# First tile of a cross-attention and FP4-FFN kernel: order of its start and placing of POOL's weight rounding

## The reference

```
x = x + xattn(layernorm(x), ctx)     # ctx (4, 154, 192), 16 heads of 64
    q = x @ Wq;  k = ctx @ Wk;  v = ctx @ Wv
    out = softmax(q k^T / 8) v;  out @ Wo + bo
x = x + ffn(layernorm(x))            # hidden size 704
    gate = fp4(x) @ fp4(w_gate)^T;  up = fp4(x) @ fp4(w_up)^T
    h = silu(gate) * up;  fp4(h) @ fp4(w_down)^T
fp4(v): scale = max|block of 16| / 6; nearest of 0, .5, 1, 1.5, 2, 3, 4, 6 times sign times scale
```

## Time and profile before

| what | us |
|---|---|
| median of 3 runs | 884.25 |
| the profiled execution | 883.6 |
| its span, first to last instruction | 881.8 |
| busy: DVE | 709.8 |
| busy: POOL | 541.3 |
| busy: ACT | 524.4 |

### The profile page before, as it was taken

How to read it: one execution, slowest core, us unless ns; L and a number is a source line. 1 busy time by engine, 2 the same in 40 slices (tenths; PEclk the granted TensorE clock), 3 DMA queues, 4 the chain that set the end, 5 groups by cost and what they waited for, 6 DMA issues and landing times.

```text
span 881.8 us, 19215 instructions
## 1 busy us (share of the span) xinstructions
PE 837.9 (95%) x6310; PEld 809.9 (92%) x6310; DVE 709.8 (80%) x2155; ACT 524.4 (59%) x1868; POOL 541.3 (61%) x810
## 2 busy tenths in 40 slices
PE   7877899999999999999999999999999999999986
PEld 6756899999988999999988999999989999999985
DVE  3888788877787888887867888887877888888887
ACT  3654566666665666666655666666665666666531
POOL 3758677764645666666553667665644567666644
PEclk7999999999999999999999999999999999999998
DMA  5301000002010000002010000000200000000000
GB/s 158 121 24 45 7 19 13 25 8 60 8 49 19 14 25 14 25 14 55 13 50 19 13 19 13 25 14 15 59 7 19 13 13 26 13 19 13 7 7 19
DMA packets 20756, 24.30 MB, mean 28 GB/s; under 512 B 2061, under 2 KB 18869, under 8 KB 20661
## 3 DMA queue, kind: packets, MB, share of 16 engines
q1 hardware_dynamic: 19573, 22.04, 8.7%
q10 hardware_dynamic: 1088, 1.05, 0.4%
HBM read 18.89 MB, written 4.19 MB: 26 GB/s over the span
## 4 chain that ended last, share of the span: by engine, by line
PE 79%; DVE 13%; issue 2%; POOL 2%; ACT 2%; DMA 1%; SPq 0%; DVEq 0%; ACTq 0%
PE ps_g L1328 12%; PE ps_s L1281 10%; PE ps_q L1235 10%; PE ps_t L1293 7%; PE ps_o L1310 7%; PE ps_o L1308 7%; PE ps_o L1309 7%; PE ps_m L1159 3%; PE ps_m L1342 3%; PE ps_m L1344 2%; PE ps_m L1343 2%; PE ps_g L1193 2%; PE ps_g L1182 2%; DVE negmax L905 2%; PE ps_q L1193 1%
## 5 line engine op out<-in xcount | busy, mean ns | idle before, releaser
L515 POOL TENSOR_TENSOR probs<-probs,rsum 128x308 f32<-128x308 f32 x256 | 180.6, 706 | 227.6 <-DVE rsum L888 227.1
L666 ACT ACTIVATE probs<-ps_s,negmax 128x154 f32<-128x154 f32 x512 | 195.1, 387 | 201.4 <-DVE negmax L905 199.8
L905 DVE TENSOR_REDUCE negmax<-ps_s 128x2 f32<-128x308 f32 x256 | 120.8, 472 | 81.1 <-PE ps_s L1281 80.3
L1308 PE MATMUL ps_o<-B_sb,pT_lo 128*128 128x256 f32 x640 | 181.3, 283 | 0.9 <-DVE x_both L1009 0.6
L1310 PE MATMUL ps_o<-B_sb,pT_hi 128*128 128x256 f32 x640 | 181.2, 283 | 0.0
L1309 PE MATMUL ps_o<-B_sb,pT_hi 128*128 128x256 f32 x640 | 180.9, 283 | 0.0
L779 DVE TENSOR_TENSOR pT_lo<-ps_t,pT_hi 128x256 fp32r<-128x256 f32 (+1 forms) x256 | 122.6, 479 | 31.3 <-ACT pT_hi L593 31.1
L1328 PE MATMUL ps_g<-WGU,xqT_hi 128*128 128x352 f32 x504 | 132.0, 343 | 1.9 <-DVE B_sb L779 1.7
L1293 PE MATMUL ps_t<-ident,probs 128*128 128x128 f32 x640 | 113.2, 275 | 13.5 <-DVE pT_lo L779 11.2
L1308 PEld LDWEIGHTS ps_o<-B_sb,pT_lo 128*128 128x128 f32 x640 | 121.3, 190 | 1.5 <-issue 0.8
L1310 PEld LDWEIGHTS ps_o<-B_sb,pT_hi 128*128 128x128 f32 x640 | 121.9, 191 | 0.0
(11 more groups left out here) (230 smaller groups left out, 2199.0 us busy)
## 6 DMA issues: line engine op xcount, KB each, us to landing
xa<-in_x_dram SPq DMA_DIRECT2D x33, 128.0 KB, 2.2
xr<-in_x_dram SPq DMA_DIRECT2D x32, 128.0 KB, 2.0
out_dram<-y_xn SPq DMA_DIRECT2D x30, 128.0 KB, 1.7
W_sb<-in_L_xattn_Wk_dram SPq DMA_DIRECT2D x3, 768.0 KB, 5.7
W_sb<-in_L_xattn_Wv_dram SPq DMA_DIRECT2D x2, 768.0 KB, 5.5
probs<-in_L_xattn_Wq_dram ACTq DMA_DIRECT2D x4, 256.0 KB, 5.5
Wo_sb<-in_L_xattn_Wo_dram SPq DMA_DIRECT2D x1, 1024.0 KB, 6.4
W_sb<-in_L_xattn_Wv_dram SPq DMA_DIRECT2D x2, 384.0 KB, 3.7
```

Of the source, the lines that this page charges most:

```text
L515: pool.tensor_tensor(unit, unit, rsum[:, 2 * u:2 * u + 2].unsqueeze(2) .to_broadcast([P, 2, M]), ALU.mult).then_inc(norm_p, 1)
L666: ins = act.activation(probs[:, h, 0:M], ps_s[k % 2][:, s * M:(s + 1) * M], ACT.Exp, bias=negmax[:, h:h + 1], accum_out=sums[:, h:h + 1])
L905: dve.tensor_reduce(negmax[:, 2 * k:2 * k + 2], ps_s[k % 2][:, 0:UM].rearrange("p (h m) -> p h m", h=2), AX_X, ALU.max, negate=True).then_ ...
L1308: pe.matmul(ps_o[:, 0:C], lo[:, j, :], w[:, 0:C], start=first, stop=False)
```

## The change

- PE runs no idle products between K's first product and the transposes of x.
- ACT and DVE split x ahead of K's first job; they had it behind.
- q of tile pair 0, unit 1, goes to the bank `ps_s[1]`, which the scores of slot 1 use later, and no longer waits for the low part of unit 0. Unit 2 now waits for the low part of unit 0, and the following units wait as before.
- POOL runs the three stages of chunks 0 to 4 in one go, one slot after RAW_AT, right behind the normalise of that slot; nothing of chunk 4 is left for the next tile's slot 0.

```
--- before.py
+++ after.py
@@ -212,6 +212,10 @@
 
         def q_slots(t, par):
             return {k: k + 2 for k in range(PAIRS - 2)} if isinstance(t, int) and t == 0 else Q_SLOTS[par]
+
+        def q_bank(pair, u):
+
+            return ps_s[1] if pair == 0 and u == 1 else ps_q
 
         def q_unit(t, par, k):
             return q_slots(t, par).get(k)
@@ -503,10 +507,10 @@
             pool.wait_ge(pre_mm, CTX_T)
             pool.memset(VT[:, :, :], 0.0).then_inc(pad_p, 1)
 
-            def round_chunk(c, stages):
+            def round_chunk(c):
                 n = RAW_N[c]
                 fp4(raw[RAW_IN[c]][:, 0:n], raw_c[c % 2][:, 0:n], raw_s[c % 2][:, 0:n // BLOCK], raw_p, 3 * c,
-                    (raw_v, 6 * c + 6), stages)
+                    (raw_v, 6 * c + 6))
 
 
             def normalise(t, u):
@@ -527,12 +531,10 @@
             def first(t, setup):
                 for k in range(SLOTS):
                     normalise(t, k)
-                    if raw_at(t, k, 2) is not None:
-                        round_chunk(raw_at(t, k, 2), (2,))
                     if t == 0 and k == 0:
                         rstd(mv1, rs1, nm1, (ln1_v, 9), ln1_p, 8)
                     if raw_at(t, k, 1) is not None:
-                        round_chunk(raw_at(t, k, 1), (0, 1))
+                        round_chunk(raw_at(t, k, 1))
                     if k == 1:
                         add_bias(t)
                     if k == 3:
@@ -552,8 +554,8 @@
                         normalise(e, PAIRS - 1)
                     if own and k >= 1:
                         normalise(t, k - 1)
-                    if raw_at(t, k, 2) is not None:
-                        round_chunk(raw_at(t, k, 2), (2,) if raw_at(t, k, 2) == raw_at(1, 0, 2) else range(3))
+                    if raw_at(t, k, 2) is not None and (t, k) != (1, 0):
+                        round_chunk(raw_at(t, k, 2))
                     if own and k == 0:
                         add_bias(t)
                     if down and 1 <= k < 4:
@@ -593,7 +595,7 @@
                 act.activation(dst, src, ACT.Copy).then_inc(done, 1)
 
             def q_hi_part(pair, u):
-                hi_part(q_sb[0][:, u, :], ps_q[:, 0:2 * P], (q_mm, PAIRS * pair + u + 1), q_hi)
+                hi_part(q_sb[0][:, u, :], q_bank(pair, u)[:, 0:2 * P], (q_mm, PAIRS * pair + u + 1), q_hi)
 
             def take_hi(job, b):
                 kind, i, bank_ = job
@@ -642,8 +644,8 @@
                 context(r)
             wq_hi_part(0)
             layer_norm1_out(1, 1)
+            hi_part(xT_all(0), parts(ps_m, 4), (xT_mm, 1), xT_hi)
             take_hi(("K", 0, FIRST_K[0]), 0)
-            hi_part(xT_all(0), parts(ps_m, 4), (xT_mm, 1), xT_hi)
             wq_hi_part(1)
             q_hi_part(0, 0)
             wq_hi_part(2)
@@ -779,7 +781,7 @@
                 dve.tensor_tensor(dst, src, hi.bitcast(F32), ALU.subtract).then_inc(done, 1)
 
             def q_lo_part(pair, u):
-                lo_part(q_sb[1][:, u, :], ps_q[:, 0:2 * P], q_sb[0][:, u, :], (q_hi, PAIRS * pair + u + 1), q_lo)
+                lo_part(q_sb[1][:, u, :], q_bank(pair, u)[:, 0:2 * P], q_sb[0][:, u, :], (q_hi, PAIRS * pair + u + 1), q_lo)
 
             def take_lo(job, b):
                 kind, i, bank_ = job
@@ -868,8 +870,8 @@
             layer_norm1(0, 0, 1)
             layer_norm1(1, 1, 1)
             wq_lo_part(0)
+            lo_part(xT_all(1), parts(ps_m, 4), xT_all(0), (xT_hi, 1), xT_lo)
             take_lo(("K", 0, FIRST_K[0]), 0)
-            lo_part(xT_all(1), parts(ps_m, 4), xT_all(0), (xT_hi, 1), xT_lo)
             wq_lo_part(1)
             q_lo_part(0, 0)
             wq_lo_part(2)
@@ -1228,11 +1230,13 @@
                     pe.wait_ge(xT_lo, pair + 1)
                 if isinstance(pair, int) and pair == 0:
                     pe.wait_ge(wq_lo, u // 2 + 1)
-                if some(PAIRS * pair + u):
+                if pair == 0 and u == 2:
+                    pe.wait_ge(q_lo, 1)
+                elif q_bank(pair, u) is ps_q and some(PAIRS * pair + u):
                     pe.wait_ge(q_lo, PAIRS * pair + u)
                 terms = [(w, x_, k) for k in range(KT) for w, x_ in ((1, 0), (0, 1), (0, 0))]
                 for i, (w, x_, k) in enumerate(terms):
-                    ins = pe.matmul(ps_q[:, 0:2 * P], Wq_sb[w][:, k, u * P:(u + 1) * P], xT[x_][:, k, :],
+                    ins = pe.matmul(q_bank(pair, u)[:, 0:2 * P], Wq_sb[w][:, k, u * P:(u + 1) * P], xT[x_][:, k, :],
                                     start=(i == 0), stop=(i == len(terms) - 1))
                 ins.then_inc(q_mm, 1)
 
@@ -1255,7 +1259,6 @@
             context_transposes(range(2))
             pe.wait_ge(pre_ev, 2)
             make(("K", 0, FIRST_K[0]), 0)
-            warm(4)
             pe.wait_ge(xln1_a, 2)
             m_free(None, (xT_lo, 1))
             both_transposes(ps_m)
```

## The result

The changed kernel takes 877.54 us, the median of 4 runs (876.86 to 878.03), against 885.01 for the kernel before measured beside it (four runs): a ratio of 0.9918, 95% interval 0.990 to 0.9936. On two other chips the same kernel gave 0.9941 (0.9923 to 0.9959) and 0.9948 (0.9934 to 0.9961). So it is faster by 0.5 to 0.8%, some 5 to 7 us. The direction held; two terms of the sum were too small.

What follows compares the result with a forecast made beforehand. TensorE (PE), busy 838 of 881.8 us, was taken to pace the steady tile pairs. The front's 2.1 us plus 2.0 us from rounding in one go made 4.1, taking the median from 884.25 to about 880.1; range 877.9 to 883.0.

Steps and rivals of the forecast that it cites:

- the front: First tile up to DVE's second maximum: that maximum moves from 27.25 to 25.15, a gain of 2.1 us.
- the collision: Slots 7 and 8: DVE's scaling of chunk 5's maxima starts inside POOL's multiplication of chunk 4 and is blocked, 0.87 us lost.
- K 0's end and the half clock: First tile: K 0 still ends at 11.17; transposes and q products run at half clock, which rises near 17.5.
- the upper bound: First tile: full clock throughout, DVE's own queue sets the first maximum near 17.7, and the gain there is 3.0 us.
- The clock rival: First tile: the clock rises at 12.95 after all, gain 3.0 + 2.0 to 2.9, time 878.8; chance 0.15.
- The second bank: First tile: q 1 no longer waits for the subtraction of q 0, so 1.01 us go.
- Slots 7 and 8: Chunk 3's earlier multiplication removes DVE waits of 1.69 and 1.21 us (2.90); less 0.87 blocked, gain 2.0 us.
- Slot 5's wait: Slot 5: PE loses its 1.63 us wait for chunk 2, worth nothing because DVE had not been idle.
- The lead stays: After the first tile: a microsecond gained stays gained unless a later wait is pinned to something else.
- The slower rival: Five moved POOL multiplications each block a DVE step by 1.24 us, 6.2 lost against 5.0 gained: 885.4; chance 0.08.

Runs made afterwards that it cites:

- cold: The changed kernel without the 12 idle products at its very start: 880.12 us, ratio 0.9957.
- one_bank: The changed kernel with q 1 back in the bank of q 0: 881.11 us, ratio 0.9962.
- nudge_long: The changed kernel with a DVE clear of 512 columns ahead of the scaling of chunk 5's maxima: 877.94 us, one run.
- filled_6: The changed kernel with idle products in two PE waits, 6 ahead of K 0 and 5 ahead of q 0: 877.40 us, ratio 0.9925.
- after_third: The changed kernel, unchanged, measured again beside filled_6 and nudge_long: 879.19 us, ratio 0.9948.
- filled: The changed kernel with idle products in two PE waits, 8 ahead of K 0 and 5 ahead of q 0: 877.69 us, ratio 0.9927.
- idle_back: The changed kernel with the four idle products back ahead of the transposes of x: 879.94 us, ratio 0.9940.
- nudge: The changed kernel with a DVE clear of 64 columns ahead of the scaling of chunk 5's maxima: 878.96 us, ratio 0.9937.
- front_only: The changed kernel with POOL's rounding as in the kernel before: 881.33 us, ratio 0.9956.
- before_filled: The kernel before with idle products in the same two PE waits as the changed kernel's filled variants: 883.60 us, ratio 0.9991.

## Why the prediction was wrong

Two terms of the sum failed: the front (2.1 us forecast, 4.3 measured) and the collision (0.87 us lost by forecast, nothing measured).

- **K 0's end and the half clock: what failed in the front.** The forecast held that "K 0 still ends at 11.17: it waits for a load that is untouched", and ran the transposes and the q products at half. The wait for Wk is untouched, but the level of the clock belongs to the execution and not to the kernel: K 0 ended at 10.29. With x transposed in 0.66 instead of 1.11 us, q 0 in 0.99 instead of 1.64 and the K products in 1.21, the front gave 4.32 us where 2.1 stood: 3.72 of them by the first maximum (1.65 forecast), 0.60 from there to the second (0.43 forecast). Even the upper bound, 3.0, kept K 0's half-clock end; adding 0.88 and 0.45 us gives 4.3. cold, whose K 0 and q 0 have the lengths of the half clock, returned the forecast's front within 0.2 us: the steps were right, the level was not. The other side of the subtraction had the same fault. The profile of before had caught a full stretch from 12.95 to 16.35 us; with the half clock throughout, the old front takes 18.9 us and not 18.1, and the order is worth 3.1 us. By this comparison the rest of the 4.3 is luck of the two executions that were profiled. One step inside was also off: PE did not run on unbroken behind q 0, it waited 0.83 us for q 0's low part ahead of the scores.
- **The clock rival** was given 0.15 and priced too low for the same reason. In the first profile after the clock never fell in the front, which is more than the rival supposed; in the three profiles of the changed kernel K 0 was at full clock each time, q in two of three. Why a level is met is only in part shown: PE was idle 2.05 and 2.33 us ahead of K 0 in the two profiles of the kernel before, 1.13 to 1.46 in the three of the changed one, and that pause hangs on the landings of context and Wk; but one_bank had 2.56 us there, nudge_long 2.19, and K 0 at full clock. How often either kernel meets the half level is left open. The Trainium skill, "TensorE: Matmul & The Clock Gate", Part 1, holds that idleness brings the throttle back. filled_6's profile agrees (pauses of 0.78 and 0.30 us, full clock), but so did two profiles of the changed kernel with pauses of 1.1 to 1.5 us, so that the products were needed is not shown. It does not follow either that the four removed idle products had helped: they stood where PE had work to do, and delayed it.
- **The second bank** was right in kind, too small in size: 1.01 us of wait; put back, 1.8 to 1.9 us of front and 2.4 us of the kernel's time. What the step left out is that in those profiles the half clock lasted 3 us longer behind the wait.
- **Slots 7 and 8: 2.0 us forecast, 3.0 measured.** The stall, the two waits and the landing of chunk 5 went as worked out (2.90). The collision term of 0.87 was wrong: it did not occur in eleven of the twelve profiles with the new rounding, and in nudge_long only because it was made to. This failure is no luck; all eleven profiles agree. The forecast had the multiplication start at 65.9 and the scaling at 66.05; in fact the scaling starts first, by 0.12 to 0.14 us in all eleven. Both chains start at the end of one DVE step (L831), so their distance is fixed and not chance; an estimate good to 0.1 us can't tell on which side it falls. The Trainium skill, "SBUF — State Buffer", has the lock as exclusive and held for the whole instruction; nudge_long agrees, with a wait to 0.03 us behind the multiplication's end.
- **How much of the miss is luck.** With the collision term at nothing the forecast is 5.0 us, which is what the two repeats gave (5.2 and 4.6). The 7.3 us of the first measurement also had the highest median of before (885.01; 883.95 to 884.59 elsewhere).
- **Slot 5's wait** was worth nothing, as said: the lead stays 4.05 us from the fifth to the eighth maximum.
- **The lead stays**: mostly right. 7.07 us became 6.57 at the last maximum.
- **The slower rival** (collisions behind the moved multiplications) did not decide, but slots 1 to 6 were not free of cost. From the second to the eighth maximum the five profiles with the old rounding took 33.2 to 33.8 us, eleven of the twelve with the new one 33.3 to 34.1, after_third 35.6. In filled, filled_6, idle_back and nudge, DVE waited 0.5 to 0.7 us for the split of chunk 0's transposes, with PE at half clock just before. What after_third met is of the same kind; its lock was with an add that had not moved against DVE, and front_only, with the old rounding, met that lock too.

## What to carry to other kernels

Read TensorE's clock level in every stretch you shift, and price the shift at both levels from the first instruction on, not from the first one that is edited; compare profiles at the same level before you credit a change with the difference. A pause that you close may pay twice. An idle product ahead of ready work delays it; whether idle products inside a wait pay is suggested here and not shown. Where two engines' instructions come within 0.2 us of each other, carry both outcomes of the meeting, or shift one of them in a test. When a dependent chain is cut in one place, look for the next in line: taking the idle products out was worth nothing alone, and 3.1 us of the front together with x ahead and a second bank. A multiplication that sits on a queue behind an instruction that waits for something else costs that whole wait; move it ahead of the wait.

## What the runs showed that I had not expected

- The new front took 13.4 to 14.3 us in the three profiles of the changed kernel and 15.8 at half, in front_only, where it is the same; runs of the changed kernel spread by up to 3 us, about half of the change's gain. In after_third a lock of 1.27 us, a PE wait of 2.46 us, nearly seven microseconds at half clock and a DVE wait of 1.56 us followed each other; how much each caused the next is not shown.
- The same load of chunk 5 needed 1.7 or 3.35 us from the end of its issue to its use (before and before_filled). The new rounding issues it about 4 us earlier, counted from the eighth maximum, and DVE needs it 2.8 us after the end of the issue. That was enough in all twelve profiles; a load of 3.35 us would still be 0.5 us late.
- A small clear of 0.11 us behind a reduction cost nothing (6.30 against 6.29 us): there was room for it in the gap that follows the reduction.
